# A state-space convolution with a routed low-rank layer: the odd blocks of x arrive by 128-byte pieces and are turned on VectorE

## The reference

```
u_m = x * mask
k   = 2 * real(einsum('hn,hnl->hl', Cs, exp(dtA * l)))       # l = 0..1023, per head
y   = (causal_conv(u_m, k) + u_m * D) * mask
logits = einsum('bsd,ed->bse', y, route_w)                   # 8 experts
weight = one_hot(argmax(logits)) * max(logits)
h   = einsum('bsd,erd->bser', y, A)
out = x + einsum('bser,eor->bso', weight * h, Bw)
```

## Time and profile before

| | us |
|---|---|
| median of 3 runs | 623.53 (622.24 to 623.84) |
| the profiled execution | 623.93 |
| its span in the trace | 622.1 |

### The profile page before, as it was taken

One profiled execution on the slowest core, in us unless ns is written; L12 is line 12 of the kernel. 1 busy time (PEld: TensorE's weight loads), 2 busy tenths in 40 slices (PEclk: granted clock), 3 DMA queues, 4 the chain that ended last, 5 costly groups with the idle time before them and its releaser, 6 DMA issues.

```text
span 622.1 us, 13886 instructions
## 1 busy us (share of the span) xinstructions
PE 591.5 (95%) x3681; PEld 530.9 (85%) x3681; DVE 542.5 (87%) x1436; ACT 379.3 (61%) x1164; POOL 372.9 (60%) x474
## 2 busy tenths in 40 slices
PE   3379999999999999999999999999999999999995
PEld 2268998999899889988998998899899989988984
DVE  7778889988988898899889888988998898889874
ACT  3676656766676666567666766665676667666520
POOL 4465566557656755675576567556755765676520
PEclk9989999999999999999999999999999999999998
DMA  6023534453454345435534543454345345434521
GB/s 137 17 56 108 152 110 128 147 150 96 142 149 132 113 139 153 112 126 146 152 96 139 151 133 110 141 152 114 125 146 152 98 136 151 139 105 140 154 78 67
DMA packets 37074, 77.68 MB, mean 125 GB/s; under 512 B 11836, under 2 KB 20350, under 8 KB 36998
## 3 DMA queue, kind: packets, MB, share of 16 engines
q1 hardware_dynamic: 27846, 43.76, 29.5%
q10 hardware_dynamic: 9152, 33.03, 13.0%
HBM read 43.16 MB, written 33.62 MB: 123 GB/s over the span
## 4 chain that ended last, share of the span: by engine, by line
PE 92%; DVE 4%; issue 2%; POOL 1%; ACT 0%; DMA 0%; POOLq 0%
PE psYo L987 19%; PE psZ L1009 19%; PE psO L987 15%; PE psYe L987 12%; PE psS L987 11%; PE psO L1036 5%; PE psXe L1000 4%; PE psXo L1000 4%; PE psZ L1078 1%; PE psS L1047 1%; DMA logs<-in_L_cond_log_dt_dram 0%; DVE ex L693 0%; POOL Grev L436 0%; POOL wave L426 0%; DVE fraction L803 0%
## 5 line engine op out<-in xcount | busy, mean ns | idle before, releaser
L468 POOL TENSOR_TENSOR Slo<-Sf,Shi 128x384 fp32r<-128x384 f32 x64 | 64.9, 1015 | 210.1 <-ACT Shi L590 210.1
L852 DVE SCALAR_TENSOR_TENSOR brought<-Sf,tab,psS 64x128 f32<-64x128 f32 x256 | 89.0, 348 | 47.3 <-ACT Sf L585 40.9
L1009 PE MATMUL psZ<-Wt,Y 128*128 128x136 f32 x1024 | 129.6, 280 | 0.0
L1009 PEld LDWEIGHTS psZ<-Wt,Y 128*128 128x128 f32 x1024 | 127.8, 191 | 0.1
L531 ACT ACTIVATE Ghi<-Grev 128x256 fp32r<-128x256 f32 x64 | 26.8, 418 | 94.2 <-POOL Grev L436 94.2
L884 DVE TENSOR_TENSOR ost<-psO,xt 128x512 f32<-128x512 f32 x128 | 82.0, 676 | 2.2 <-PE psO L987 2.2
L461 POOL TENSOR_TENSOR Xlo<-xeven,Xhi 128x512 fp32r<-128x512 f32 x64 | 82.8, 1293 | 0.0
L568 ACT ACTIVATE Xhi<-psXe 128x512 fp32r<-128x512 f32 x64 | 38.2, 597 | 38.3 <-PE psXe L1000 38.3
L789 DVE TENSOR_SCALAR whole<-turns_t 128x256 f32<-128x256 f32 x64 | 57.8, 903 | 4.1 <-ACT turns_t L519 4.1
L585 ACT ACTIVATE Sf<-psS 128x128 f32<-128x128 f32 x64 | 17.7, 277 | 66.4 <-PE psS L987 66.4
L987 PE MATMUL psYo<-Xhi,Thi 128*128 128x512 f32 x128 | 55.6, 434 | 0.0
(11 more groups left out here) (194 smaller groups left out, 1670.8 us busy)
## 6 DMA issues: line engine op xcount, KB each, us to landing
xt<-in_x_dram SPq DMA_DIRECT2D x64, 512.0 KB, 4.1
out_dram<-ost ACTq DMA_DIRECT2D x63, 512.0 KB, 4.8
Traw<-kdram SPq DMA_DIRECT2D x64, 128.0 KB, 2.9
kdram<-krow SPq DMA_DIRECT2D x64, 1.0 KB
A_nat<-in_L_ffn_A_dram SPq DMA_DIRECT2D x1, 512.0 KB, 4.9
B_nat<-in_L_ffn_Bw_dram SPq DMA_DIRECT2D x8, 64.0 KB, 3.6
out_dram<-ost SPq DMA_DIRECT2D x2, 256.0 KB, 2.0
lens_i<-in_itok_B_dram SPq DMA_DIRECT2D x1, 64.0 KB, 3.6
```

Of the source, the lines that this page charges most:

```text
L468: pool.tensor_tensor(Slo[h.s2][:, :], Sf[h.s2][:, :], Shi[h.s2][:, :].bitcast(F32), ALU.subtract).then_inc(slo_done, 1)
L852: dve.scalar_tensor_tensor(brought[to, :], Sf[h.s2][fr, old], tab2[fr, BR, h.n:h.n + 1], psS[to, new], ALU.mult, ALU.add).then_inc(brought ...
L1009: last = pe.matmul(psZ[:, 0:NW], Y[:, j, c, :], Wt[:, 2 * c + j, :], start=(j == 0 and c == 0), stop=(j == 1 and c == NE - 1), skip_group_ ...
```

## The change

The odd blocks of x are no longer turned by PE. SP loads them a second time, with 16 more DMAs for each head, each of 32 partitions by 4 pieces by 32 numbers (128 pieces of 128 bytes, 16 KB). They land in a new tile `xblk` such that position group g (32 positions) of the block is on partitions 32g to 32g + 31 by sequence, and one VectorE transpose of 32x32 squares over 128x512 turns all odd blocks of the head into `xodd` in SBUF. `Xhi` of the odd blocks is then made on ScalarE from `xodd` and not from PSUM, and before the even one and not behind it. `Xlo` of the odd blocks moves from VectorE to GpSimd. The four PE transposes of odd blocks are gone. `xt` is loaded whole as before, since the even blocks and `add` need it.

```diff
+            def load_blocks(h):
+
+                need(sp, xodd_done, h.n - 1)
+                for g in range(G4):
+                    for c in range(NE):
+                        sp.dma_start(xblk[h.s2][g * G32:(g + 1) * G32, c, :, :],
+                                     bass.AP(x.tensor, h.n * L + c * Q + P + g * G32,
+                                             [[H * L, G32], [G32 * H * L, G4], [1, G32]])
+                                     ).then_inc(blk_in[h.s2], 16)
...
             def step(head):
                 if head(2).there:
+                    load_blocks(head(2))
                     load_x(head(2))
                     write_kernel(head(2))
                     skew_kernel(head(2))
...
+            load_blocks(Head(0))
             with nc.allow_non_contiguous_dma(reason="expert rows of 16"):
...
             load_x(Head(1))
+            load_blocks(Head(1))
             sp.wait_ge(pad_done, 32)
...
+            def x_lo_odd(h):
+
+                need(pool, xhi_odd, h.n + 1)
+                need(pool, y_mm, (h.n - 1) * 2)
+                pool.tensor_tensor(Xlo[h.s2][:, 1, :], xodd[:, :], Xhi[h.s2][:, 1, :].bitcast(F32),
+                                   ALU.subtract).then_inc(xlo_odd, 1)
...
-                    x_hi(head(1), 0)
-                    x_hi(head(1), 1)
+                    x_hi_odd(head(1))
+                    x_hi_even(head(1))
...
+            def turn_blocks(h):
+
+                need(dve, blk_in[h.s2], (h.half + 1) * 16 * G4 * NE)
+                need(dve, xlo_odd, h.n)
+                dve.transpose(xodd[:, :], xblk[h.s2][:, :, :, :].rearrange("p c g i -> p (c g i)")
+                              ).then_inc(xodd_done, 1)
...
             def step(head):
+                if head(1).there and not is_head(head(0), 0):
+                    turn_blocks(head(1))
                 if head(0).there:
                     carry(head(0))
...
-                if head(1).there and not is_head(head(0), 0):
-                    x_lo(head(1))
...
-            def turn_x(h, j):
+            def turn_x(h):
...
-                    turn_x(head(1), 0)
-                    turn_x(head(1), 1)
+                    turn_x(head(1))
```

More of the change, by code:

```diff
@@ L40, in conv_ffn_kernel @@
     G16 = 16
+    G32 = 32
+    G4 = P // G32
     assert B == P and 2 * N == P and ER == P and HALF == 512 and H % 8 == 0
@@ L117, in conv_ffn_kernel @@
         xeven = sb("xeven", [P, HALF])
+        xblk = [sb(f"xblk{s}", [P, NE, G4, G32]) for s in range(2)]
+        xodd = sb("xodd", [P, HALF])
         turns_h = [sb(f"turns_h{s}", [P, Q]) for s in range(2)]
@@ L225, in conv_ffn_kernel @@
         xt_done = sem("xt_done")
-        xhi_done = sem("xhi_done")
+        blk_in = [sem(f"blk_in{s}") for s in range(2)]
+        xodd_done = sem("xodd_done")
+        xhi_even = sem("xhi_even")
+        xhi_odd = sem("xhi_odd")
         xeven_done = sem("xeven_done")
@@ L471, in step @@
             def step(head):
+                if head(1).there:
+                    x_lo_odd(head(1))
                 if head(0).there and not is_head(head(0), 0):
@@ L487, in _ @@
             x_lo(first[0])
+            x_lo_odd(first[0])
             pool.wait_ge(mag_done, 2)
@@ L563, in t_hi, with x_hi_even, x_hi_odd @@
                                ACT.Copy).then_inc(thi_done, 1)
-            def x_hi(h, j):
-                need(act, xt_done, h.n * 2 + j + 1)
+            def x_hi_even(h):
+                need(act, xt_done, h.n + 1)
                 need(act, y_mm, (h.n - 1) * 2)
-                act.activation(eo(Xhi[h.s2], j), psX[j][:, :], ACT.Copy).then_inc(xhi_done, 1)
+                act.activation(eo(Xhi[h.s2], 0), psX[0][:, :], ACT.Copy).then_inc(xhi_even, 1)
+            def x_hi_odd(h):
+                need(act, xodd_done, h.n + 1)
+                need(act, y_mm, (h.n - 1) * 2)
+                act.activation(eo(Xhi[h.s2], 1), xodd[:, :], ACT.Copy).then_inc(xhi_odd, 1)
             def x_even(h):
@@ L626, in _ @@
             first = [Head(n) for n in range(4)]
-            x_hi(first[0], 0)
-            x_hi(first[0], 1)
+            x_hi_even(first[0])
             x_even(first[0])
@@ L632, in _ @@
                            ACT.Copy).then_inc(tab_done, 1)
+            x_hi_odd(first[0])
             act.wait_ge(phases_done, 1)
@@ L668, in _ @@
             m_matrix(first[2])
-            x_hi(first[1], 0)
-            x_hi(first[1], 1)
+            x_hi_odd(first[1])
+            x_hi_even(first[1])
             x_even(first[1])
@@ L771, in _ @@
             e1, e256 = er[:, 0:N], er[:, N:2 * N]
+            turn_blocks(Head(0))
             dve.wait_ge(den_set, 1)
@@ L804, in clamp @@
                                   ALU.max, ALU.min).then_inc(frac_done, 1)
[L806 to L811, removed]
             def largest(h):
@@ L950, in _ @@
             whole_turns(first[1])
-            x_lo(first[0])
             fractions(first[1])
@@ L973, in _ @@
                    Bw_hi[:, j * 512:(j + 1) * 512].bitcast(F32), ALU.subtract).then_inc(blo_set, 1)
+            turn_blocks(first[1])
             dve.wait_ge(mask_done, NB)
@@ L990, in three @@
                 return mm
-            def turn_x(h, j):
+            def turn_x(h):
                 need(pe, x_in[h.s4], h.quarter * 16 + 16)
-                need(pe, *((xlo_odd, h.n) if j else (xeven_done, h.n)))
+                need(pe, xeven_done, h.n)
                 if is_head(h, 1):
-                    pe.wait_ge(krow_done, j + 1)
+                    pe.wait_ge(krow_done, 1)
                 for c in range(NE):
-                    at = (2 * c + j) * P
-                    last = pe.transpose(psX[j][:, c * P:(c + 1) * P], xt[h.s4][:, at:at + P], ident[:, :])
+                    at = 2 * c * P
+                    last = pe.transpose(psX[0][:, c * P:(c + 1) * P], xt[h.s4][:, at:at + P], ident[:, :])
                 last.then_inc(xt_done, 1)
@@ L1015, in bring @@
             def bring(h):
-                need(pe, xhi_done, h.n * 2 + 2)
+                need(pe, xhi_even, h.n + 1)
+                need(pe, xhi_odd, h.n + 1)
                 need(pe, xlo_even, h.n + 1)
@@ L1043, in turn_k @@
                 need(pe, krow_done, h.n)
-                if h.n < 2:
-                    need(pe, *((xlo_odd, 1) if h.n else (xeven_done, 1)))
+                if h.n == 0:
+                    need(pe, xeven_done, 1)
                 need(pe, s_carried, (h.n - 1) * 2)
@@ L1126, in _ @@
             pe.wait_ge(consts, 10)
-            turn_x(first[0], 0)
-            turn_x(first[0], 1)
+            turn_x(first[0])
             pe.wait_ge(pack1_done, 1)
```

## The result

The changed kernel takes 845.2 us (836.02 to 850.72 in 4 runs), the kernel before 623.68. The ratio is 1.351, with a 95% interval from 1.340 to 1.362: slower by a third. The forecast was 741 us. A ratio leaves out executions that took over 1.5% longer than the fastest of their kernel.

What follows compares the result with a forecast made beforehand. PE bounds the kernel before; SP's queue would bound the changed one: 6.72 + 0.38 + 3.42 + 0.37 = 10.89 us a head. 42.9 + 1.5 + 61 x 10.89 + 30.5 + 1.8 = 741 us; own range 695 to 831, wide 640 to 845.

Steps and rivals of the forecast that it cites:

- The loop on SP: SP queue, each head: sixteen block loads, x, the `krow` wait and `Traw` run in order, 10.89 us against 8.99 before.
- `krow` wait: SP queue: `krow` lands only when x ahead of it has landed, a wait of 3.42 us, against 1.17 without queueing.
- the pitch of an issue: SP queue: each block load takes 0.42 us from issue to issue, sixteen of them 6.72 us a head.
- The start: Before the first steady `krow`: block loads ahead of `B_nat` and the first `krow` add 1.5 us, between 0 and 7.
- the tail: After the last steady `krow`: 30.5 us, unchanged by the edit.
- Rival two: VectorE, held by GpSimd's new subtraction for up to 1.0 us, becomes the bound: 9.36 us a head, 648 us; 7%.
- Hidden, with one side effect: GpSimd: the added 1.29 us ahead of `Slo` fits where it idled 3.25 us; the side effect is a VectorE hold.
- Rival one: SP queue: `krow` isn't held behind x, so SP's loop is 8.64 us and the time 603 us; 10%.
- Rival three: DMA engines become the bound if packets cost 73 ns: 13.3 us a head, 888 us; hidden at 11.5 ns; 6%.
- The transpose: VectorE: the 32x32 transpose of 128x512 takes 0.68 us, as much as the subtraction that VectorE loses.
- PE's idle time: PE: idles about 2.3 us a head, most of it for the DMA of `xt`.
- PE's clock: PE: at 79% busy its clock may fall in part; at 0.77 all along, 13 us more at most.

Runs made afterwards that it cites:

- the loads alone: Kernel before with the sixteen block loads added on SP into a tile nobody reads, PE still turning the odd blocks: 832.9 us, ratio 1.335.
- x ahead of them: Changed kernel with the load of x issued ahead of the sixteen block loads on SP: 806.0 us, ratio 1.291.
- one load: Changed kernel with one load of 256 KB in 2 KB rows replacing each head's sixteen block loads, odd blocks getting wrong elements: 802.7 us, ratio 1.287.
- the kernel with 6 issues moved and the two moves: Changed kernel, x loaded first, late odd subtraction, 6 of 16 block loads on ScalarE's queue, `xeven` ahead of `Shi`, `whole` behind both masked `Y`: 674.6 us.
- one load and the late subtraction: Changed kernel with one 256 KB load for the sixteen, and GpSimd's odd subtraction behind the even one, not ahead of `Slo`: 670.5 us, ratio 1.074.
- one more subtraction: Kernel before with only an added GpSimd subtraction of 128x512 for each head, ahead of `Slo`: 708.6 us, ratio 1.136.

## Why the prediction was right in direction and too small

**The loop on SP: right, as a mechanism.** The forecast named its four terms. Measured in the kernel after: `krow` wait 3.33 (forecast 3.42), `Traw` 0.39 (0.37), x 0.57 with its gap (0.38), sixteen pitches of 0.512, 8.19 (6.72). That makes 12.48 of the 12.61 us. The two experiments on SP confirm it: the loads alone give 12.40, and x ahead of them takes the wait away. The start (44.15 against 42.86, 1.3 us for a forecast of 1.5) and the tail (842.4 - 813.3 = 29.1, forecast 30.5) were right too.

**The term that was mis-sized: the pitch of an issue.** I took 0.42 us between the 0.38 of an isolated issue and 0.47. The line of the block loads in the kernel after says what it is: 432 ns median, up to 1803, to which comes the gap of 0.05. The steady row of 0.33 was of an issue before which SP had idled; back to back, 0.43 was the rule, as two rows at the start had shown, and some issues take 0.7 to 1.8 us. 0.09 us in sixteen issues in 61 heads are 90 us, and 0.19 on x are 12 more: that is the 104 us between 741 and 845, near enough. The measured time lies above the forecast's own range, which ended at 831, and at the very edge of the wide one. That edge, 845, had been drawn up "a little" without a term for it, so that it nearly holds the result is luck.

**Rival two was real, and priced far too low.** It was given 7% and 9.36 us a head. The mechanism, VectorE held until a GpSimd instruction ends, is what the runs show, but at 11.9 us. I had counted one held instruction; there are three with one load, and in the changed kernel `Sf` too. And I had priced it as busy time of VectorE, where it lies on a path that PE waits for, with PE's clock lower in part of the heads. In the changed kernel it hides behind SP's loop all but 0.2 us a head (12.61 against 12.40 with the loads alone), so the forecast of the time hardly suffered; the sentence "Hidden, with one side effect" did. The Trainium skill has the rule (SBUF — State Buffer, "Who interferes with whom"): a VectorE instruction in a two-port mode, or one with two SBUF inputs beside a GpSimd instruction that reads SBUF, and the GpSimd instruction exclude each other for the whole instruction, whichever comes first. The rows agree as to which are held: `frac` and `Sf`, with two SBUF inputs, and `fraction` and `gate` are, while `brought`, `Y` and `Blo`, which read PSUM, keep their times (348 ns mean for `brought`, before and after). In which mode `fraction` and `gate` ran, no trace shows.

**Rival one** (no queueing behind x) fell: 3.33 us with x ahead of `krow`, 1.42 without. **Rival three** (DMA engines as the bound) fell: between 412 and 416 us of the kernel after the queue moved 1412 packets, nearly all of 128 bytes, at 29.5% of 16 engines, 13 ns a packet. **The transpose** was 0.71 us (forecast 0.68). **PE's idle time** is there for `xt` (95.4 us), as forecast, and for `wh` (87.8), which was not. **PE's clock** fell in part, as the forecast left room for (0.919 as a mean of the run).

## What to carry to other kernels

Count the DMA issues of a queue as work of an engine, at their back-to-back pitch (here 0.50 to 0.51 us whether a DMA moves 32 or 128 pieces), and add the waits between them: a queue that waits most of the time can become the bound through many small loads. Idle time of GpSimd is not free room: look at which VectorE instructions run beside it and whether they touch PSUM, and at who waits for them. When the holds are gone, GpSimd's added time can still lie in a loop through ScalarE and `carry`, as it did here. And where two bounds lie close, undo each alone before believing in one, since either explains most of the loss.

## What the runs showed of the hardware that was not expected

- One 1.3 us GpSimd subtraction, placed in GpSimd's own idle time, made the kernel before 85 us slower (10.38 against 9.00 us a head).
- Even a VectorE instruction over 128x8 numbers is held for as long as GpSimd's runs: `gate`, 302 ns before, 1020 in the kernel with one load. The 32x32 transpose is not: 696 to 714 ns over 64 executions, and in the kernel with 6 issues moved and the two moves, where it always runs beside a GpSimd instruction, 698 ns as a mean.
- Loads in 128-byte pieces with 256 KB between rows cost the DMA engines 13 ns a piece, hardly more than the 11.5 ns of 64-byte pieces from dense memory.
- With `krow` two packets long, an x load of 512 KB ahead of it on the same queue moved its landing from 1.2 to 3.3 us.
- With PE idle for 2.44 us once a head (the kernel with one load), the granted clock fell in about every second head, to 0.87 as a mean of the head; with 0.96 us once a head (one load and the late subtraction) it stayed at 0.988 over the whole run, with 1.20 (one more subtraction) at 0.997.
